# Attention reads the turned x back from DRAM, and the K projection is split around the second sums

## The chip, the cores and the metric

The kernel runs on one core of one Trainium2 chip. Its time is the device time of one execution in microseconds; lower is better. Three timed runs of the kernel before are shown, and one more execution was taken with the hardware profiler.

## What is computed

One decoder layer in float32 with 64 sequences of 128 tokens, width D = 256, 16 heads of 16. Three blocks, each with a residual and a layer norm behind it. Cut to what matters:

```python
# recurrence, per token t, with x [64, 128, 256]
q, k, v = x @ Wq, x @ Wk, x @ Wv;  g = sigmoid(x @ Wf + bf)
state = state * g + v outer k;      out = state @ q
out = layernorm(out) * gamma + beta
x1 = layernorm(x + (out * silu(x @ Wg)) @ Wout)
# cross attention with ctx [64, 128, 256]
Q, K, V = x1 @ Wxq.T + bq, ctx @ Wxk.T + bk, ctx @ Wxv.T + bv
x2 = layernorm(x1 + (softmax(Q K^T / 4) V) @ Wxo.T + bo)
# feed-forward with fake quantization: its outputs are scaled and rounded by the maximum over all tokens
x3 = layernorm(x2 + ffn(x2))
```

## The kernel before, in words

Three blocks of code follow one another, with all engines meeting between them: `recurrence_block`, `attention_block`, `feedforward_block`. In each block every engine has a program of its own, written out by hand, and the engines wait for one another on semaphores (counters). Within an engine the instructions run strictly in the written order, so a wait holds up everything behind it on that engine. There is no scheduler.

The first two blocks work on pairs of sequences, 32 pairs (`NP`). A matmul contracts over the partitions, so x has to be turned (features on the partitions, tokens along the row) before it is multiplied with a weight.

- The recurrence loads x of pair p into `rec_x`, turns it on TensorE (`turn`, four 128x128 transposes into a PSUM bank), and ScalarE copies the result to `rec_xT` (`turned`). The second sequence of a pair lies in `rec_x` and `rec_xT` with its four chunks of 32 tokens in reverse order (`place`). The result `rec_o` goes to the DRAM tensor `rec_scratch` (`store`), one DMA of 128 rows and four of 32.
- Attention loads three tiles of a pair in `load`: `att_x` from the input x, `att_ctx` from the context, `att_o` from `rec_scratch`. All three count up one semaphore of the slot, `a_loaded`, by 16 each. There are two slots. SyncE (SP) issues the load of a pair into a slot once `x1` of the pair that used the slot two pairs earlier is ready, that is, when VectorE has written both halves of `att_x1`.

In attention a step p handles the front half of pair p (gate, output of the recurrence, x1, K and V of the context) and the scores, softmax and output of pair p-1. TensorE's order in a steady step, by its helpers: turn x of pair p (`turn4(F[0], xs)`), turn the normalized recurrence output (`on`), the sums and values of the second sequence left from the step before (`values(n0-1)`: matmuls of the exponentials with ones and with V; "the second sums" are these), turn x1 of pair p-1, K projection of pair p (`across(F[1], wx[:, 1], cT)`), query projection, output projection (`att_out`), scores, gate projection (`across(F[2], w_g, xT)`), V projection, the second pass over the scores (`probs`, which needs the row maxima of VectorE through a transpose of `mparts`), the product with `w_out` (which needs `att_yT` of VectorE), scores, sums and values of the other sequence, the turn of the next context, `probs`, `att_out`.

VectorE's order in a step: `att` (the quotient of the sequence before), `stats_o` and `apply_o` of the pair p+1 (they read `att_o`, so they wait for `a_loaded`), `residual` and `stats2`, `maxima` of the first sequence, the gate's product `att_yT`, V, residual, `maxima` of the second sequence, `att`, statistics of x1, `residual`, and `apply`, which writes `att_x1` and so frees the slot for the next load.

Of the kernel before, what the change touches and what calls it, by code (L numbers as in the profile page):

```python
# [24 lines left out]
P = 128  # L25
# [47 lines left out]
def recurrence_block(nc, t, w, x_d, o_d):  # L73
# [25 lines left out]
    with ExitStack() as ctx:  # L99
# [60 lines left out]
        stored = [sem(f"rec_stored{i}") for i in range(2)]  # L160
        names = """marked consts consts_ready x_made xT_ready vf_made v_ready z_ready ez_ready lg_ready h_ready n_ready q_made q_ready
# [31 lines left out]
        with nc.Block() as block:  # L193

            @block.sync
            def _(sp):
# [12 lines left out]

                for s in range(2):  # L210
                    sp.sem_inc(stored[s], DMAS)
# [19 lines left out]
                sp.wait_ge(q["x_made"], 1)  # L231
                load(2, 0)
# [5 lines left out]
                sp.wait_ge(q["x_made"], NP - 2)  # L238
                load(NP - 1, 1)
                for p in range(NP - 4, NP):  # L240
                    store(p, p % 2)
                sp.wait_ge(qw["rest_loaded"], 16 * 12)
# [262 lines left out]
            def _(act):  # L505
# [245 lines left out]
def attention_block(nc, t, x_d, ctx_d, o_d):  # L751
# [3 lines left out]
    with ExitStack() as ctx:  # L755
# [12 lines left out]
        xT = sb("att_xT", [P, KC, 2 * P])  # L768
# [38 lines left out]
        names = """xT_made xT_ready cT_made cT_ready x1T_made x1T_ready q_made q_ready zg_made th_ready sg_ready  # L807
# [25 lines left out]
        with nc.Block() as block:  # L833

            @block.sync
            def _(sp):
                def load(pair, slot):
                    two = bass.ds(2 * pair, 2)
                    for dst, src in ((xs, x_d), (cs, ctx_d), (os_, o_d)):
                        sp.dma_start(dst[:, slot], src[two].rearrange("b t d -> t b d")).then_inc(a_loaded[slot], 16)  # L840

                load(0, 0)
                load(1, 1)
                with sp.Fori(0, (NP - 2) // 2) as j:
                    for u in range(2):
                        sp.wait_ge(q["x1_ready"], 2 * (2 * j + 1 + u))
                        load(2 * j + 2 + u, u)

            @block.tensor
            def _(pe):  # L850
# [12 lines left out]
                def across(bank_, wt, rhs, done):  # L863

                    for oc in range(KC):
# [3 lines left out]
                    m.then_inc(done, 1)  # L869
# [72 lines left out]
                def turn_context(p, s, before):  # L942
                    pe.wait_ge(a_loaded[s], 48 * (before + 1))
                    wait_if(pe, q["v_ready"], p)
                    turn4(F[1], cs[:, s], q["cT_made"])

                def step(p, s, before, front, attn, tail):
# [3 lines left out]
                    if front:  # L951
                        pe.wait_ge(a_loaded[s], 48 * (before + 1))
# [31 lines left out]
                    if front:  # L984
                        pe.wait_ge(q["ogb_ready"], 2 * p + 2)
                        pe.wait_ge(q["xT_ready"], p + 1)
                        across(F[2], t["w_g"], xT, q["zg_made"])
# [21 lines left out]
            def _(act):  # L1009
# [27 lines left out]
                def step(p, s, before, front, attn, tail):  # L1037
                    n0 = 2 * p - 2
                    if front:
                        act.wait_ge(q["xT_made"], p + 1)  # L1040
                        A.activation(flat(xT), F[0][:], ACT.Copy).then_inc(q["xT_ready"], 1)
# [42 lines left out]
            def _(dve):  # L1084
# [86 lines left out]
                def stats_o(p, s, before):  # L1171
                    dve.wait_ge(a_loaded[s], 48 * (before + 1))
# [743 lines left out]
def decoder_layer(nc, x_d, ctx_d, w, out_d):  # L1916

    with ExitStack() as ctx:
# [6 lines left out]
        r_d = nc.dram_tensor("raw_scratch", (NT, P, FC * 512), F32).ap()  # L1925
        g_d = nc.dram_tensor("gate_scratch", (NT, P, FC * 512), F32).ap()
# [9 lines left out]
        with ExitStack() as early:  # L1936
# [16 lines left out]
            recurrence_block(nc, t, w, x_d, o_d)  # L1953
            attention_block(nc, t, x_d, ctx_d, o_d)
# [28 lines left out]
```

## Time and profile before

| | us |
|---|---|
| median of 3 timed runs | 2223.21 (2216.39 to 2224.17) |
| profiled execution | 2219.33 |
| its span in the trace | 2217.6 |
| TensorE busy | 2007.4, 91% of the span |
| VectorE busy | 1582.9, 71% |
| ScalarE busy | 1268.4, 57% |
| mean granted TensorE clock | 0.962 of full speed |

The recurrence ends at about 772 us of the span, attention runs from about 773 to 1545 us, and the feed-forward block fills the rest. The profile names an engine's instruction by its line and by the tiles it writes and reads (out<-in). A number in square brackets behind a row is the time in which the engine stood idle before that row, with the instruction that ended the wait. PE is TensorE, PEld its weight loads, DVE VectorE, ACT ScalarE, POOL GpSimd, SPq the DMAs that SyncE issues. A float32 matmul shows as two records, a float32 transpose as one.

### The profile page before, as it was taken

The page shows a single profiled execution, that of the slowest core. Times are in us where ns is not written, and L with a number is a line of the kernel's source. Part 1 is how long each engine was busy: PE and PEld are TensorE (multiplying, and loading weights), DVE is VectorE, ACT ScalarE, POOL GpSimd, SP SyncE. Part 2 cuts the span into 40 slices and gives each one's busy share as a digit, 9 for nine tenths or more (in the row PEclk, how much of TensorE's full clock was granted, in tenths as well). Part 3 has the DMA queues.
Part 4 walks back from the last instruction along what each step waited for, and adds up shares of the span by engine and source line. Part 5 has one row for each costly group of instructions (what it writes and reads, how often), then busy time and mean ns, then how long its engine had stood idle before and what let it go on. Part 6 is the DMA issues. An engine that isn't in the chain of part 4 may idle for free. (4 is left out here: it accounts for less than half of the span.)

```text
span 2217.6 us, 72815 instructions
## 1 busy us (share of the span) xinstructions
PE 2007.4 (91%) x29431; PEld 1367.3 (62%) x29431; DVE 1582.9 (71%) x2810; ACT 1268.4 (57%) x2047; POOL 314.4 (14%) x313
## 2 busy tenths in 40 slices
PE   7999999999999789999999999997777877889798
PEld 4666666666666567777777777775333423334587
DVE  6787867777677757677677776775333379988897
ACT  4445444544445356766767667664544467678565
POOL 1231100101010111111111111110000022300021
PEclk9899999999999889999999999998888989999999
DMA  3001010100100010100101001000222368869574
GB/s 115 22 24 30 22 32 22 32 22 26 28 22 27 26 48 30 43 28 28 43 28 42 29 28 43 28 29 1 103 119 119 142 245 309 292 261 424 211 265 161
DMA packets 87527, 196.80 MB, mean 89 GB/s; under 512 B 11059, under 2 KB 64566, under 8 KB 87350
## 3 DMA queue, kind: packets, MB, share of 16 engines
q1 hardware_dynamic: 87350, 194.03, 24.7%
q8 instruction: 161, 2.64, 0.5%
q14 instruction: 16, 0.13, 0.0%
HBM read 108.01 MB, written 85.98 MB: 87 GB/s over the span
## 5 line engine op out<-in xcount | busy, mean ns | idle before, releaser
L1340 PE MATMUL ff_twin<-ff_xq,w_uh 128*128 (+1 forms) x1152 | 356.7, 392 | 42.7 <-DVE ff_top L1722 36.4
L1340 PEld LDWEIGHTS ff_twin<-ff_xq,w_uh 128*128 128x128 f16 x1152 | 113.5, 101 | 192.5 <-issue 55.4
L1340 PE MATMUL ff_twin<-ff_xq,w_ul 128*128 (+1 forms) x576 | 224.0, 389 | 0.0
L537 ACT ACTIVATE x<-rec_e,rec_hidden 128x512 f32<-128x512 f32 x256 | 156.0, 702 | 36.6 <-PE rec_e L372 36.6
L1119 DVE TENSOR_REDUCE mneg<-att_s 128x4 f32<-128x512 f32 x256 | 159.0, 684 | 17.8 <-PE att_s L894 17.1
L653 DVE TENSOR_TENSOR x<-rec_x,rec_until 128x512 f32<-128x512 f32 x256 | 158.8, 683 | 17.8 <-PE rec_x L356 17.8
L384 PE MATMUL rec_x<-x 32*32 32x64 f32 x8192 | 147.0, 219 | 18.1 <-DVE x L653 12.1
L384 PEld LDWEIGHTS rec_x<-x 32*32 32x32 f32 x8192 | 126.2, 107 | 54.6 <-issue 54.5
L1732 DVE TENSOR_REDUCE ff_top<-ff_out 128x1536 f32 (+1 forms) x32 | 56.1, 1754 | 137.0 <-ACT ff_out L1473 137.0
L1022 ACT ACTIVATE att_e<-att_s 128x512 f32<-128x512 f32 x256 | 132.2, 602 | 36.5 <-PE att_s L914 36.5
L333 PE MATMUL rec_f<-w_rec,rec_xT 128*128 128x512 f32 x256 | 134.9, 652 | 5.6 <-DVEq L586 4.5
L341 PE MATMUL rec_f<-rec_xT,w_rec 128*128 128x256 f32 x512 | 138.2, 404 | 0.9 <-ACT rec_v L519 0.9
L1782 DVE TENSOR_TENSOR ff_out<-ff_whole,s_other 128x1536 f32<-128x1536 int16 x64 | 115.0, 1802 | 27.3 <-ACT s_other L1527 14.0
L689 DVE TENSOR_TENSOR rec_tmp<-rec_x,x 32x256 f32<-32x256 f32 (+1 forms) x192 | 80.8, 421 | 75.2 <-PE rec_x L412 50.4
L289 POOL TENSOR_TENSOR rec_o<-rec_tmp 128x512 f32<-128x512 f32 x32 | 41.1, 1283 | 632.1 <-DVE rec_tmp L706 632.1
L1241 POOL TENSOR_TENSOR rs<-mv,half_pow 128x1 f32<-128x1 f32 (+1 forms) x96 | 57.8, 602 | 477.4 <-DVE mv L1163 379.1
L683 DVE TENSOR_TENSOR rec_tmp<-rec_x,x 128x512 f32<-128x512 f32 x128 | 83.8, 683 | 50.1 <-PE rec_x L384 49.9
L537 ACT ACTIVATE x<-rec_e 128x512 f32<-128x512 f32 x64 | 38.1, 597 | 131.6 <-PE rec_e L372 131.6
L341 PEld LDWEIGHTS rec_f<-rec_xT,w_rec 128*128 128x128 f32 x512 | 90.8, 192 | 33.3 <-issue 11.0
L1786 DVE TENSOR_REDUCE ff_topg<-ff_out 128x1536 f32 (+1 forms) x64 | 110.0, 1741 | 0.2 <-DVE ff_coef L1770 0.2
L1340 PEld LDWEIGHTS ff_twin<-ff_xq,w_ul 128*128 128x128 f16 x576 | 57.8, 100 | 72.1 <-issue 9.7
L676 DVE TENSOR_TENSOR x<-x,rec_v 128x2048 f32<-128x2048 f32 x32 | 73.3, 2291 | 37.4 <-ACT x L537 37.4
(250 smaller groups left out, 4481.7 us busy)
## 6 DMA issues: line engine op xcount, KB each, us to landing
raw_scratch<-ff_out SPq DMA_DIRECT2D x32, 768.0 KB, 3.2
ff_in<-raw_scratch SPq DMA_DIRECT2D x32, 768.0 KB, 6.0
gate_scratch<-ff_out SPq DMA_DIRECT2D x28, 768.0 KB, 3.6
ff_in<-gate_scratch SPq DMA_DIRECT2D x28, 768.0 KB, 9.1
product_scratch<-ff_out SPq DMA_DIRECT2D x28, 768.0 KB, 8.6
ff_out<-product_scratch SPq DMA_DIRECT2D x28, 768.0 KB, 6.2
att_x<-in_x SPq DMA_DIRECT2D x32, 256.0 KB, 2.7
att_ctx<-in_ctx SPq DMA_DIRECT2D x32, 256.0 KB, 2.9
```

What stands on the lines that cost most here:

```text
L333: T.matmul(bank_[:], xT[:, kc, b * P:(b + 1) * P], wr[:, kc, 2:4].rearrange("p a d -> p (a d)"), start=(kc == 0), stop=False)
L341: m = T.matmul(bank_[:, oc * 2 * P:(oc + 1) * 2 * P], wr[:, kc, i, oc * P:(oc + 1) * P], xT[:, kc], start=(kc == 0), stop=(kc == KC - 1))
L384: m = T.matmul(X[k][rows(c), h * NR * HD:(h + 1) * NR * HD].rearrange("p (r i) -> p r i", r=NR), mt[rows(c), b, hd, rows(c)], e[rows(c), s ...
L537: A.activation(out, E[(s + k) % 2][:], ACT.Exp, bias=hidden[:, asks, r:r + 1] if r < NR else 0.0, scale=-1.0 if asks else 1.0).then_inc(q[ ...
L653: V.tensor_tensor(mt[:, b].rearrange("p (a j m) n -> p j a m n", a=KC, m=2)[:, j], X[j].rearrange("p (a m n) -> p a m n", a=KC, m=2), unti ...
L683: V.tensor_tensor(tmp[:, k * HH:(k + 1) * HH, 0:NR], X[k].rearrange("p (h r i) -> p h r i", r=NR, i=HD), um[:, s, :, k * HH * HD:(k + 1) * ...
L689: V.tensor_tensor(tmp[lanes, b * H:(b + 1) * H, k], bank_[lanes, b * D:(b + 1) * D].rearrange("p (h i) -> p h i", i=HD), e[lanes, s, k, b ...
L1022: A.activation(e[:, b, j], X[j][:], ACT.Exp).then_inc(q["e_ready"], 1)
L1119: V.tensor_reduce(mneg[:, 4 * j:4 * j + 4], X[j].rearrange("p (h k) -> p h k", h=4), AX.X, ALU.max, negate=True).then_inc(q["s_taken"], 1)
L1340: m = T.matmul(bank_[:], weights(wp, kc, a, c), tile[:, xp, kc], start=(i == 0), stop=(i == len(terms) - 1))
L1782: V.tensor_tensor(ob[:, u, s], whole[:, u, s], other[:, s], ALU.mult).then_inc(q["prod"], 1)
L1786: V.tensor_reduce(topg[:, bass.ds(2 * k + s, 1)], ob[:, u, s], AX.X, ALU.max, apply_absolute_value=True).then_inc(q["maxed"], 1)
```

## The change

1. The recurrence writes each `rec_xT` to a new DRAM tensor `turned_scratch` (`keep`): one DMA for the first sequence (256 pieces of 512 bytes) and four for the chunks of the second, put back in order of time (256 pieces of 128 bytes each). ScalarE's copy of the next turned x waits until these have landed (`xT_out`). SyncE's order is now load, keep, store.
2. Attention no longer turns x nor copies it to `att_xT`. `load` gets a fourth DMA that reads the turned x, 128 rows of 2 KB, into a double-buffered place inside `raw_down`, a tile that is not in use then. It counts up the same semaphore, so all waits on `a_loaded` go from 48 to 64 a round.
3. Of the K projection of the next pair, the first of the two output chunks now stands ahead of `values(n0-1)`, the second stays behind the turn of x1.

```diff
+                def keep(pair):
+                    sp.wait_ge(q["xT_ready"], pair + 1)
+                    kept = xt_d[bass.ds(pair, 1)].rearrange("a p k n -> (a p) k n")
+                    sp.dma_start(kept[:, :, 0:P], xT[:, :, 0:P]).then_inc(xT_out, 16)
+                    for chunk in range(NC):
+                        at = place(1, chunk)
+                        sp.dma_start(kept[:, :, P + CH * chunk:P + CH * (chunk + 1)],
+                                     xT[:, :, P + CH * at:P + CH * (at + 1)]).then_inc(xT_out, 16)
...
                 with sp.Fori(0, NP // 2 - 2) as j:
                     for u in range(2):
-                        sp.wait_ge(q["x_made"], 2 * j + u + 2)
-                        load(2 * j + 3 + u, 1 - u)
+                        sp.wait_ge(q["x_made"], 2 * j + u + 3)
+                        load(2 * j + u + 4, u)
+                        keep(2 * j + u + 2)
                         store(2 * j + u, u)
...
                 def turned(p):
                     act.wait_ge(q["x_made"], p + 1)
+                    wait_if(act, xT_out, DMAS * p)
...
                     for dst, src in ((xs, x_d), (cs, ctx_d), (os_, o_d)):
                         sp.dma_start(dst[:, slot], src[two].rearrange("b t d -> t b d")).then_inc(a_loaded[slot], 16)
+                    sp.dma_start(xT[:, slot], xt_d[bass.ds(pair, 1)].rearrange("a p k n -> (a p) k n")).then_inc(a_loaded[slot], 16)
...
                     if front:
-                        pe.wait_ge(a_loaded[s], 48 * (before + 1))
-                        if attn and not tail:
-                            pe.wait_ge(q["xT_ready"], p)
-                        turn4(F[0], xs[:, s], q["xT_made"])
+                        pe.wait_ge(a_loaded[s], 64 * (before + 1))
...
                         turn4(F[2], on, q["onT_made"])
+                        pe.wait_ge(q["cT_ready"], p + 1)
+                        across(F[1], wx[:, 1], cT, q["k_made"], range(1))
                     if tail:
                         values(n0 - 1, s, 1)
                     if attn:
                         pe.wait_ge(q["x1_ready"], 2 * p)
-                        if front:
-                            pe.wait_ge(q["xT_ready"], p + 1)
                         turn4(F[0], x1, q["x1T_made"])
                     if front:
-                        pe.wait_ge(q["cT_ready"], p + 1)
-                        across(F[1], wx[:, 1], cT, q["k_made"])
+                        across(F[1], wx[:, 1], cT, q["k_made"], range(1, KC))
...
                 def stats_o(p, s, before):
-                    dve.wait_ge(a_loaded[s], 48 * (before + 1))
+                    dve.wait_ge(a_loaded[s], 64 * (before + 1))
```

How it moves instructions shows at three places. First TensorE at the start of a steady attention step, up to the query projection. Before (in the names, `att_x` stands for x and for x1):

```order
531 L859 MATMUL att_f<-ident,att_x 128x128 x4
532 L958 REGISTER_ALU
533 L859 MATMUL att_f<-ident,att_on 128x128 x4
534 L69 REGISTER_ALU
535 L921 ISA
536 L924 MATMUL att_a<-att_e,ones_half 32x256 x8
537 L930 MATMUL att_a<-att_e,v_half 32x128 x16
538 L966 REGISTER_ALU
539 L859 MATMUL att_f<-ident,att_x 128x128 x4
540 L867 MATMUL att_f<-att_cT,w_x 128x256 x4
541 L874 MATMUL att_f<-att_x1T,w_x 128x256 x4
```

The same place of the changed kernel:

```order
531 L876 MATMUL att_f<-ident,att_on 128x128 x4
532 L976 REGISTER_ALU
533 L884 MATMUL att_f<-att_cT,w_x 128x256 x2
534 L69 REGISTER_ALU
535 L939 ISA
536 L942 MATMUL att_a<-att_e,ones_half 32x256 x8
537 L948 MATMUL att_a<-att_e,v_half 32x128 x16
538 L876 MATMUL att_f<-ident,att_x 128x128 x4
539 L884 MATMUL att_f<-att_cT,w_x 128x256 x2
540 L892 MATMUL att_f<-att_x1T,w_x 128x256 x4
```

The first four transposes, those of x, are gone, and two of the four matmuls of the K projection have moved ahead of the sums.

Second SyncE in the attention loop, one pair's load. Before:

```order
92 L840 ISA
93 L840 DMA att_x<-in_x 128x2x256
94 L840 DMA att_ctx<-in_ctx 128x2x256
95 L840 DMA att_o<-rec_scratch 128x2x256
96 L840 ISA
```

And now (`raw_down` is where the turned x lies):

```order
122 L856 ISA
123 L856 DMA att_x<-in_x 128x2x256
124 L856 DMA att_ctx<-in_ctx 128x2x256
125 L856 DMA att_o<-rec_scratch 128x2x256
126 L857 ISA
127 L857 DMA raw_down<-turned_scratch 128x512
```

The fourth DMA stands last, behind that of `att_o`.

Third SyncE at the start of the recurrence, behind the weights. Before:

```order
25 L198 DMA rec_x<-in_x 128x256
26 L200 DMA rec_x<-in_x 32x256 x4
27 L233 UNCONDITIONAL_BRANCH
28 L233 ISA
29 L198 ISA
30 L198 DMA rec_x<-in_x 128x256
```

And now:

```order
26 L201 DMA rec_x<-in_x 32x256 x4
27 L214 DMA turned_scratch<-rec_xT 256x1x128
28 L217 DMA turned_scratch<-rec_xT 256x1x32 x4
29 L199 DMA rec_x<-in_x 128x256
30 L201 DMA rec_x<-in_x 32x256 x4
```

The five DMAs that write the turned x of pair 0 come behind the load of pair 2 and ahead of that of pair 3.

## Rows read from the trace of the kernel before

**Rows 1.** Windows: busy us of PE, PEld, DVE, ACT, POOL; granted clock; DMA.
```profile
20.00:740.00 720.00, 673.56 (x16410) 469.82 (x16410) 546.97 (x760) 345.82 (x602) 104.95 (x69) 0.98 0.10 26
800.00:1500.00 700.00, 688.59 (x8698) 519.23 (x8696) 497.33 (x1344) 478.97 (x870) 111.77 (x149) 1.00 0.11 33
```

**Rows 2.** Timeline of PE in attention: start, us, instruction, idle before it.
```profile
1101.79 1.89 PE L867 MATMUL att_f<-att_cT,w_x 128*128 128x256 f32 x8
...
1113.07 1.99 PE L882 MATMUL att_f<-w_out,att_yT 128*128 128x256 f32 x8
...
1120.38 1.13 PE L939 MATMUL att_a<-w_x,att_attT 128*128 128x256 f32 x4
1121.35 0.60 PE L859 MATMUL att_f<-ident,att_x 128*128 128x128 f32 x4
1121.79 0.60 PE L859 MATMUL att_f<-ident,att_on 128*128 128x128 f32 x4
1122.59 1.07 PE L924 MATMUL att_a<-att_e,ones_half 128*32 128x256 f32 x16 [0.20 <-ACT att_e L1022]
```

**Rows 3.** Timeline of DVE in the same step.
```profile
1104.31 0.75 DVE L1158 BATCH_NORM_STATS2 st_o<-att_o 128x6 f32<-128x256 f32 x2 [0.95 <-DMA att_o<-rec_scratch]
...
1111.31 0.23 DVE L1125 TENSOR_TENSOR mparts<-mneg,mparts 128x64 bf16<-128x64 f32 x1
...
1112.32 0.69 DVE L1202 TENSOR_TENSOR att_yT<-att_silu,att_ogb 128x512 f32<-128x512 f32 x1 [0.19 <-DVE att_silu L1198]
...
1121.89 0.73 DVE L1168 TENSOR_SCALAR att_x<-att_res,mv,rs 128x256 f32<-128x256 f32 x2
```

**Rows 4.** Timeline of SP, loads of two pairs in attention.
```profile
1100.09 0.42 SPq L840 DMA_DIRECT2D att_ctx<-in_ctx  x1
1100.61 0.42 SPq L840 DMA_DIRECT2D att_o<-rec_scratch  x1
...
1123.80 0.42 SPq L840 DMA_DIRECT2D att_o<-rec_scratch  x1
```

**Rows 5.** DMA issues of the page: count, KB each, median us from issue to landing.
```profile
att_ctx<-in_ctx SPq DMA_DIRECT2D x32, 256.0 KB, 2.9
att_o<-rec_scratch SPq DMA_DIRECT2D x32, 256.0 KB, 3.6
...
rec_scratch<-rec_o SPq DMA_DIRECT2D x128, 32.0 KB, 1.6
```

**Rows 6.** A window of 0.4 us while three tiles arrive; last columns DMA share, GB/s.
```profile
1124.60:1125.00 0.40, 0.40 (x5) 0.40 (x5) 0.35 (x1) 0.40 (x1) 0.00 (x0) 1.00 1.09 364
```

**Rows 7.** Timeline of DVE and PE in a step whose `att_o` landed early.
```profile
1126.99 0.75 DVE L1158 BATCH_NORM_STATS2 st_o<-att_o 128x6 f32<-128x256 f32 x2 [0.46 <-DMA att_o<-rec_scratch]
...
1136.13 1.99 PE L882 MATMUL att_f<-w_out,att_yT 128*128 128x256 f32 x8
```

**Rows 8.** The tile `att_o`: what its readers waited for (us, times), and landing.
```profile
  DMA att_o<-rec_scratch: 35.8, 31
...
DMA to landing us min/median/max: 3.0/3.6/4.8
```

**Rows 9.** Timelines of SP and ACT in a steady step of the recurrence.
```profile
418.32 3.34 SPq L200 DMA_DIRECT2D rec_x<-in_x  x4
...
440.68 0.63 ACT L511 ACTIVATE rec_xT<-rec_f 128x512 f32<-128x512 f32 x1
```

**Rows 10.** Timelines at the start of the recurrence: SP, ACT, PE.
```profile
21.77 1.35 SPq L200 DMA_DIRECT2D rec_x<-in_x  x3
...
26.15 0.63 ACT L511 ACTIVATE rec_xT<-rec_f 128x512 f32<-128x512 f32 x1
...
26.92 1.96 PE L333 MATMUL rec_f<-w_rec,rec_xT 128*128 128x512 f32 x4 [1.12 <-ACT rec_xT L511]
```

**Rows 11.** Windows at the end of attention, columns as in rows 1.
```profile
1520.00:1530.00 10.00, 8.15 (x90) 5.50 (x83) 6.02 (x15) 3.50 (x8) 0.77 (x2) 1.00 0.00 0
1530.00:1540.00 10.00, 9.33 (x136) 7.06 (x125) 3.33 (x7) 4.92 (x10) 0.00 (x0) 0.66 0.01 2
```

More of the change, by code:

```diff
@@ L69, in wait_if, with recurrence_block @@
         eng.wait_ge(sem, value)
-def recurrence_block(nc, t, w, x_d, o_d):
+def recurrence_block(nc, t, w, x_d, o_d, xt_d):
     NP = B // 2
@@ L160, in recurrence_block @@
         stored = [sem(f"rec_stored{i}") for i in range(2)]
+        xT_out = sem("rec_xT_out")
         names = """marked consts consts_ready x_made xT_ready vf_made v_ready z_ready ez_ready lg_ready h_ready n_ready q_made q_ready
@@ L230, in _ @@
                     sp.dma_start(t[dst][:], w[dst].partition_broadcast(P)).then_inc(qw["rest_loaded"], 16)
-                sp.wait_ge(q["x_made"], 1)
-                load(2, 0)
+                for p in range(2):
+                    sp.wait_ge(q["x_made"], p + 1)
+                    load(p + 2, p)
+                    keep(p)
                 with sp.Fori(0, NP // 2 - 2) as j:
                     for u in range(2):
-                        sp.wait_ge(q["x_made"], 2 * j + u + 2)
-                        load(2 * j + 3 + u, 1 - u)
+                        sp.wait_ge(q["x_made"], 2 * j + u + 3)
+                        load(2 * j + u + 4, u)
+                        keep(2 * j + u + 2)
                         store(2 * j + u, u)
-                sp.wait_ge(q["x_made"], NP - 2)
-                load(NP - 1, 1)
-                for p in range(NP - 4, NP):
+                for p in range(NP - 2, NP):
+                    keep(p)
+                    store(p - 2, p % 2)
+                for p in range(NP - 2, NP):
                     store(p, p % 2)
+                sp.wait_ge(xT_out, DMAS * NP)
                 sp.wait_ge(qw["rest_loaded"], 16 * 12)
@@ L746, in _, with attention_block @@
                 weights()
-def attention_block(nc, t, x_d, ctx_d, o_d):
+def attention_block(nc, t, x_d, ctx_d, o_d, xt_d):
     NP = B // 2
@@ L767, in attention_block @@
         os_ = sb("att_o", [P, 2, 2, D])
-        xT = sb("att_xT", [P, KC, 2 * P])
+        xT = t["raw_down"].rearrange("p c d -> p (c d)")[:, 0:4 * KC * P].rearrange("p (s k n) -> p s k n", s=2, k=KC)
         cT = sb("att_cT", [P, KC, 2 * P])
@@ L861, in turn4, with across @@
                     m.then_inc(done, 1)
-                def across(bank_, wt, rhs, done):
-                    for oc in range(KC):
+                def across(bank_, wt, rhs, done, chunks=range(KC)):
+                    for oc in chunks:
                         for kc in range(KC):
@@ L868, in across @@
                                          rhs[:, kc], start=(kc == 0), stop=(kc == KC - 1))
-                    m.then_inc(done, 1)
+                    if chunks[-1] == KC - 1:
+                        m.then_inc(done, 1)
                 def query(p, oc):
@@ L951, in step @@
                     if front:
[L952 to L955 removed]
+                        pe.wait_ge(a_loaded[s], 64 * (before + 1))
                         if isinstance(p, int) and p == 0:
@@ L985, in step @@
                         pe.wait_ge(q["ogb_ready"], 2 * p + 2)
-                        pe.wait_ge(q["xT_ready"], p + 1)
-                        across(F[2], t["w_g"], xT, q["zg_made"])
+                        across(F[2], t["w_g"], xT[:, s], q["zg_made"])
                         pe.wait_ge(q["k_ready"], 2 * p + 2)
@@ L1925, in decoder_layer @@
         r_d = nc.dram_tensor("raw_scratch", (NT, P, FC * 512), F32).ap()
+        xt_d = nc.dram_tensor("turned_scratch", (B // 2, P, KC, 2 * P), F32).ap()
         g_d = nc.dram_tensor("gate_scratch", (NT, P, FC * 512), F32).ap()
@@ L1952, in decoder_layer @@
             })
-            recurrence_block(nc, t, w, x_d, o_d)
-            attention_block(nc, t, x_d, ctx_d, o_d)
+            recurrence_block(nc, t, w, x_d, o_d, xt_d)
+            attention_block(nc, t, x_d, ctx_d, o_d, xt_d)
         feedforward_block(nc, t, r_d, g_d, u_d, out_d)
```

4 lines of the change are left out of this document (1 added, 3 removed).

## The prediction

> **What bounds the kernel now.** I read the windows by stage first. From 800 to 1500 us, attention, TensorE is busy 688.6 of 700 us at a granted clock of 1.00; the recurrence has it busy 673.6 of 720 us [rows 1]. So attention looks bound by TensorE alone, and every matmul taken out of it looks like time won. The timelines of a step then tell more. A steady step takes about 23.3 us. On TensorE I follow it from the end of `att_out`, 1120.38 + 1.13 = 1121.51 [rows 2]. There VectorE adds the residual and writes x1, done at 1121.89 + 0.73 = 1122.62 [rows 3]; this frees the slot, and SP issues the three loads, the one of `att_o` at 1123.80 [rows 4]. VectorE's next large piece starts with the statistics of that same `att_o`, and it stood idle for the DMA: 0.95 us in the step shown [rows 3], 35.8 us in 31 of 32 steps [rows 8]. So the load comes too late for VectorE in every step. VectorE works in order, and behind this wait stand the maxima (`mparts`, done at 1111.54) and the gate's product `att_yT` (1112.32 + 0.69 = 1113.01) [rows 3]. TensorE starts the product with `w_out` at 1113.07, 0.06 us after `att_yT` [rows 2, 3]. There is a second loop beside TensorE's own: x1, load, statistics, maxima, `att_yT`, `w_out`, the rest of the step, x1.
>
> Which of the two sets the pace shows in steps whose load landed at different times. In the usual step VectorE starts on `att_o` 3.70 us after its issue (1100.61 to 1104.31) and `w_out` follows 8.76 us later, 12.46 after the issue [rows 2 to 4]. In a step with an early landing it starts 3.19 us after the issue (1123.80 to 1126.99), but `w_out` comes 9.14 us after that, 12.33 after the issue [rows 4, 7]. So 12.33 is TensorE's own path and 12.46 that of the load. Of the 30 steps whose load is issued inside the loop, 25 keep a distance of at most 8.88 us from the start of `st_o` to `w_out` (like the first pair of rows) and five have 0.1 to 0.4 us more (like the second): the load's loop binds in 25, TensorE in five, and the two lie 0.13 us apart. That is the whole argument: TensorE is full, but not alone in setting the end.
>
> **The change part by part.** All sums are against the profiled execution, 2219.3 us (span 2217.6), which lies 3.9 us under the median of the runs, 2223.2.
>
> Turn of x removed: the four transposes hold TensorE for 1121.79 - 1121.35 = 0.44 us a step [rows 2]. ScalarE's copy to `att_xT` (0.6 us) goes too; ScalarE isn't late there. Half K projection ahead of the sums: two of four matmuls, half of 1.89 us [rows 2], moved and not saved. It covers the 0.20 us that TensorE waits for the exponentials today [rows 2], since it lasts longer than the turn that it replaces. TensorE's own path thus shrinks by 0.64 us, from 12.33 to 11.69. What is late next is the load's loop at 12.46, so of the 0.64 us nothing arrives, save in the five steps in which TensorE was last: about 0.3 us each, 1.5 us in all.
>
> The fourth load: it is issued last, about 0.5 us behind that of `att_o` (the pitch of 1100.09 to 1100.61 [rows 4]), and VectorE's statistics now wait for it as well, though they don't read it. While the three tiles arrive the DMA moves 364 GB/s, its share 1.09 [rows 6]. 256 KB more take 262 / 364 = 0.72 us at that rate. If the queue were not full, the fourth would land by its issue pitch later, 0.5 us. If it came as `att_o` comes behind `att_ctx`, it would be 0.52 + 3.6 - 2.9 = 1.2 us [rows 4, 5]. I take 0.7: the windows show a full stream, and the rate is what a further tile meets. Nothing hides it, because VectorE already idles at this wait, and everything from there to `w_out` is the fixed 8.76 us. 30 steps by 0.7 are 21.0 us; less the 1.5 us above, 19.5.
>
> (The Trainium skill, DMA: Bandwidth & Descriptors, section Anatomy of one DMA, fits a DMA as a fixed part plus its bytes at 436 GB/s. By that 256 KB add 0.60 us, and the term would be 18.0 instead of 21.0. The rate in rows 6 is lower, and the estimate above goes by it.)
>
> The first pairs of attention wait for their first load in the open; the fourth DMA adds 0.7 us once. The last step with a front half has no load behind it, and there the 0.64 us are won once.
>
> Writing the turned x, steady part: SP has issued its load by 418.32 + 3.34 = 421.66; five more DMAs at the same 0.84 us take it to 425.9, and with the 1.6 us that a 32 KB store needs to land they are there by about 427.5 [rows 5, 9]. ScalarE's next copy, which now waits for them, starts at 440.68 [rows 9]: 13 us to spare. The store of `rec_o` behind them in SP's queue waits for GpSimd's result until near the end of the step anyway, and its slot is needed two steps later. Cost 0. Without that cover each us of lateness would cost ScalarE's copy, and TensorE behind it, one.
>
> Writing it, start: SP ends the load of pair 2 at 21.77 + 1.35 = 23.12 [rows 10]. Five DMAs at about 0.5 us bring the last issue to 25.2, and landing 1.6 us or more later gives 27 [rows 5]. The copy of pair 1 starts at 26.15 today, and TensorE already waits for it [rows 10], so this delay is open. I take 1.0 us, between 0 and 2.5.
>
> Sum: 19.5 + 0.7 - 0.6 + 1.0 = **20.6 us slower**: 2239.9 for an execution like the profiled one, 2243.8 from the median. I say 2243.
>
> **The rivals.**
> (a) TensorE's path decides, as the share of 98% says. Place: the start of each step; price: 0.64 us by 31 steps, 20 us, so 2203, faster. It decides alone only if the load's loop gets 0.77 us shorter than today, since only then is 11.69 the longer path. For it speaks nothing but the busy share; against it the 0.06 us between `att_yT` and `w_out`, and that the change adds to the load rather than taking from it.
> (b) The fourth tile costs nothing: it lands together with `att_o` because that one is slow for a reason of its own (its landing varies from 3.0 to 4.8 us [rows 8]), and the DMA has room. Then the loop stays at 12.46, 1.5 + 0.6 us are won and 1.0 lost: 2222, no change. Against it the full rate [rows 6].
> (c) The clock. TensorE will idle some 1.2 us more a step, most of it ahead of the second pass over the scores. After 10 us with TensorE 8.15 us busy the clock granted in the next 10 was 0.66, which is a drop to the lower of the two levels for part of them [rows 11]. A drop costs 0.34 by 10 = 3.4 us of matmul time. If it came in half of the steps it would add 15 by 3.4 = 51 us: 2294. Against it: the steps would still be about 94% busy, and the recurrence runs at 673.6 / 720 = 94% with 0.98 granted [rows 1].
> (d) The small pieces written in the recurrence are slow and hold up ScalarE's copy in every step. 1280 pieces a pair are 80 for each of 16 DMA engines; to use up 13 us each would need over 0.16 us. A piece of 1 KB takes 16 KB / 364 GB/s = 0.05 us [rows 6]. At twice the limit, each step would lose 13 us and the kernel would be at 2600. (The Trainium skill, same page, section Specifications, says that pieces under 512 bytes are read, changed and written back, and gives no price. At double the 0.05 us the sum stays as it is.)
>
> **How the numbers follow.** Forecast 0.70, (b) or a tile that costs less than 0.35 us 0.15, (a) 0.06, (c) 0.06, (d) 0.03. The forecast's own range by the bounds of the fourth tile: 30 by 0.5 less 1.5 with a start of 0 gives 13.6 us, 2237; 30 by 1.2 less 1.5 with a start of 2.5 gives 37 us, 2261. To hold 8 in 10, the range has to take in most of (b): 2224 to 2262. About 0.5%, 11 us, is what a measurement of this kernel can tell from no change. Slower by more than that (over 2234): the forecast with (c) and (d), 0.77. Within it: (b) and a small part of the forecast, 0.17. Faster: 0.06.
>
> **What would show it.** Right: VectorE's idle time ahead of `st_o` grows from 0.95 to about 2.0 us a step (0.7 of the tile, 0.3 because ScalarE, rid of a copy, lets VectorE come to it sooner) and is put down to the new DMA; the distance from `att_o`'s issue to `w_out` goes from 12.46 to about 13.2, that from the start of `st_o` to `w_out` stays 8.76; attention's TensorE share falls from 98% to about 94%, with idle time ahead of the second pass over the scores (`mneg`, `mparts`) and ahead of `w_out`; its clock stays 1.00; the recurrence, from 60 to 740 us, keeps its length. Wrong: a period of attention below 23.3 us, or a tile landing under 0.35 us after `att_o`, or a clock under 0.98 in attention, or ScalarE waiting for `turned_scratch` beyond the first steps.

## The result, and the profile after

The changed kernel takes 2267.5 us (median of 4 runs, 2254.6 to 2271.8), against 2219.8 for the kernel before (4 runs, 2211.5 to 2224.2). The ratio is 1.021, with a 95% interval of 1.0153 to 1.0266. It is slower, as forecast, but by about 47 us where 20.6 were forecast, and the time lies outside the range, whose upper end was 2262. A second measurement of the same kernel (the first experiment below) confirms the size.

First the windows by stage, with the columns of rows 1.

```profile
60.00:740.00 680.00, 641.39 (x15702) 447.74 (x15700) 512.99 (x707) 322.58 (x560) 104.47 (x68) 0.97 0.15 36
800.00:1500.00 700.00, 689.22 (x8048) 500.86 (x8046) 464.15 (x1259) 434.29 (x791) 104.41 (x139) 0.98 0.14 44
```

TensorE's busy share in attention is 689.2 of 700, as high as the 688.6 of rows 1. By this number alone nothing has happened. But it did fewer matmuls in that time (8048 against 8698, 7.5% less, while the removed transposes are only 4 of some 290 in a step), and the clock is 0.98 instead of 1.00. Short waits inside a group of matmuls are counted as busy, as shown below, so this share can't show the longer loop. The counts and the timelines can.

The loads of one pair, from SP's timeline, then VectorE's timeline of the same step:

```profile
1123.10 0.37 SPq L856 DMA_DIRECT2D att_x<-in_x  x1
1123.57 0.42 SPq L856 DMA_DIRECT2D att_ctx<-in_ctx  x1
1124.09 0.42 SPq L856 DMA_DIRECT2D att_o<-rec_scratch  x1
1124.69 0.34 SPq L857 DMA_DIRECT2D raw_down<-turned_scratch  x1
```

```profile
1129.08 0.75 DVE L1169 BATCH_NORM_STATS2 st_o<-att_o 128x6 f32<-128x256 f32 x2 [2.66 <-DMA raw_down<-turned_scratch]
...
1136.07 0.23 DVE L1136 TENSOR_TENSOR mparts<-mneg,mparts 128x64 bf16<-128x64 f32 x1
1137.09 0.69 DVE L1213 TENSOR_TENSOR att_yT<-att_silu,att_ogb 128x512 f32<-128x512 f32 x1 [0.19 <-DVE att_silu L1209]
```

These answer to rows 3 and 4. VectorE comes to the statistics and idles 2.66 us for the new DMA. What the readers of `att_o` wait for, and when that tile itself has landed:

```profile
  DMA raw_down<-turned_scratch: 81.9, 31
...
DMA to landing us min/median/max: 3.4/3.7/4.7
```

VectorE waited 35.8 us in 31 steps [rows 8]; now it is 81.9 us, all of it put down to the fourth tile. The 3.7 us for `att_o` are no proof that this tile lands as before: all four DMAs count on one semaphore, and landings are read from its counts.

TensorE's timeline over two steps:

```profile
1107.96 2.49 PE L926 MATMUL att_s<-att_qm,att_kT 32*128 32x256 f32 x8
...
1111.73 3.55 PE L900 MATMUL att_f<-w_out,att_yT 128*128 128x256 f32 x8 [0.25 <-DVE att_yT L1213]
...
1134.07 2.49 PE L926 MATMUL att_s<-att_qm,att_kT 32*128 32x256 f32 x8
...
1137.83 1.99 PE L900 MATMUL att_f<-w_out,att_yT 128*128 128x256 f32 x8 [0.25 <-DVE att_yT L1213]
```

In the second step `w_out` starts at 1137.83, 8.75 us after `st_o` at 1129.08: the fixed distance of the prediction. The group of L926 is the first half of the second pass over the scores, eight matmuls that wait for VectorE's maxima (`mneg`). They take 2.49 us; in the kernel before they take 0.71, because `mneg` is there already:

```profile
1111.29 0.71 PE L908 MATMUL att_s<-att_qm,att_kT 32*128 32x256 f32 x8
```

The 1.8 us between the two lengths are idle time, but not one idle stretch. TensorE gets two matmuls at a time, one pair for each `mneg`, 0.6 us apart. Its weight loads show the waits, and a window over the same time counts PE as fully busy, because each matmul's record lasts 0.37 to 0.48 us and reaches over the wait behind it:

```profile
1108.56 0.29 PEld L926 LDWEIGHTS att_s<-att_qm,att_kT 32*128 32x128 f32 x2 [0.30 <-DVE mneg L1130]
1109.16 0.29 PEld L926 LDWEIGHTS att_s<-att_qm,att_kT 32*128 32x128 f32 x2 [0.31 <-DVE mneg L1130]
...
1108.00:1110.50 2.50, 2.50 (x9) 1.23 (x9) 2.43 (x6) 0.00 (x0) 0.00 (x0) 1.00 0.00 0
```

I call this the thin stretch. In the first step the product with `w_out` (L900) takes 3.55 us instead of 1.99, and two windows of 4 us show why:

```profile
1108.00:1112.00 4.00, 3.75 (x34) 2.14 (x35) 3.74 (x9) 0.78 (x3) 0.00 (x0) 1.00 0.00 0
1112.00:1116.00 4.00, 4.00 (x32) 2.84 (x35) 1.76 (x5) 2.84 (x5) 0.00 (x0) 0.57 0.00 0
```

From 1112 to 1116 us, shortly behind the thin stretch, the granted clock is 0.57, so for most of them it was at the lower of the two levels (1.2 of 2.4 GHz). The trace has nine such drops in the attention loop, and each comes 3.4 to 4.2 us after the start of this group, about when `w_out` begins.

I measured both distances of the prediction over all 30 loads issued inside the loop. From the issue of `att_o` to the start of `st_o` it is 3.71 us on average before and 4.82 after. From `st_o` to `w_out` it is 8.76 or 8.88 in 23 of 30 steps before and in 27 after. From `st_o` to the issue of the next `att_o` it is between 19.4 and 19.7 in most steps of both; after the change it is about 21.2 in 8 of 29, and in the first step, which has the ninth drop, 19.65, where the first and the fifth experiment below, without a drop there, have 17.96. So the 52.2 us by which the profiled executions differ (span 2269.8 against 2217.6) are made up as follows. The loop, from the first to the last of these issues, holds 29 steps and is 44.1 us longer. Its third line is what the first two leave; the filled kernel below, without a drop, has 2.6 there.

| place | us |
|---|---|
| recurrence, with its start | +1.8 |
| attention loop, `st_o` starts later behind the issue: 29 × 1.10 | +31.9 |
| attention loop, nine clock drops: 9 × 1.65 | +14.9 |
| attention loop, the rest: steps that TensorE had bound, and a shorter first step | −2.7 |
| first pair of attention | +1.1 |
| behind the last load, 3.8 of it in feed-forward | +5.3 |

The first line of the table can't be told from nothing: the six traces here whose recurrence is the unchanged one reach attention between 767 and 773 us.

### The profile page after: what moved, and what is told of

It is laid out like the page before. It is cut to its first block and busy times, and to the rows that moved or that the text cites. A ratio compares the mean times of both kernels' runs of the same rounds, so it can differ in the third digit from the quotient of the medians.

```text
span 2269.8 us, 73055 instructions
## 1 busy us (share of the span) xinstructions
PE 2057.5 (91%) x29303; PEld 1378.4 (61%) x29303; DVE 1581.0 (70%) x2810; ACT 1250.1 (55%) x2015; POOL 314.7 (14%) x313
## 5 line engine op out<-in xcount | busy, mean ns | idle before, releaser
L1351 PE MATMUL ff_twin<-ff_xq,w_uh 128*128 (+1 forms) x1152 | 361.3, 397 | 43.6 <-DVE ff_top L1733 35.2
L926 PE MATMUL att_s<-att_qm,att_kT 32*128 32x256 f32 x1024 | 148.1, 430 | 3.2 <-DVE mneg L1130 2.9
```

The source lines that it names most:

```text
L926: T.matmul(X[j][:, oc * 2 * P:(oc + 1) * 2 * P].rearrange("p (m q) -> p m q", m=2), kT[rows(j), s, oc, toks], qm[rows(j), oc, :, toks], st ...
L1351: m = T.matmul(bank_[:], weights(wp, kc, a, c), tile[:, xp, kc], start=(i == 0), stop=(i == len(terms) - 1))
```

## The experiments

Ratios are against the kernel before, run beside each experiment on the same chip. "Lag" is the mean from the issue of `att_o` to the start of `st_o`; "loop" is from the first to the last of these loads' issues, 676.5 us before and 720.6 after.

**The changed kernel once more.** No edit.

> The changed kernel itself, once more, beside the others of this chip: 44 to 52 us slower than the kernel before. The clock theory expects again some 6 to 12 of the 30 loop steps to be 1.6 us longer than the rest, and mean granted clock in attention 0.97 to 0.99.

2261.7 us, ratio 1.0207 (1.0172 to 1.0242). Lag 4.74, loop 715.4, seven clock drops in it, each in a step of 21.2 to 21.4 us, and the clock of attention again below 1:

```profile
800.00:1500.00 700.00, 690.28 (x8062) 503.05 (x8060) 468.05 (x1269) 433.52 (x789) 105.51 (x141) 0.98 0.14 43
```

Both parts of the loss in the loop are there again, so neither is an accident of one execution.

**The turned x on a semaphore of its own.** The load is the same, but only TensorE waits for it, right ahead of the gate projection.

```diff
-sp.dma_start(xT[:, slot], ...).then_inc(a_loaded[slot], 16)
+sp.dma_start(xT[:, slot], ...).then_inc(t_loaded[slot], 16)
-dve.wait_ge(a_loaded[s], 64 * (before + 1))    # statistics; the same for TensorE's turns
+dve.wait_ge(a_loaded[s], 48 * (before + 1))
+pe.wait_ge(t_loaded[s], 16 * (before + 1))
 across(F[2], t["w_g"], xT[:, s], q["zg_made"])
```

> The changed kernel, with one thing altered: the load of the turned x counts up a semaphore of its own, on which TensorE waits ahead of the gate projection; VectorE's statistics wait for three tiles as before the change. All the traffic and TensorE's new order stay. Theory (the fourth tile at VectorE's wait costs about 1.1 us a step, and the clock drops that follow from TensorE idling cost the rest): from the issue of att_o to the start of its statistics 3.7 us again instead of 4.8, steps of about 23.2 us, granted clock in attention 0.99 to 1.00, in all within 5 us of the kernel before. Rival (the writes to DRAM in the recurrence, the missing turn or the split K projection cost by themselves): it stays 20 to 50 us slower than the kernel before.

2228.3 us, ratio 1.0093 (1.0057 to 1.0128). More than half of the loss goes once VectorE's statistics no longer wait for a tile that they don't read. It doesn't go altogether: 17 us are left by the medians and 21 by the ratio, so the expectation, within 5 us, was missed. The loop is 8.3 us longer than before (684.8) and the lag is 4.00; the rest lies outside the loop and is not broken down. One step of the loop is long, though the clock of attention rounds to 1.00. The page's DMA issues, with size and median time to landing, say what is left:

```profile
att_o<-rec_scratch SPq DMA_DIRECT2D x32, 256.0 KB, 4.0
raw_down<-turned_scratch SPq DMA_DIRECT2D x32, 256.0 KB, 4.0
```

Here the three tiles that VectorE waits for are alone on their semaphore, so the landing can be trusted: `att_o` lands at 4.0 instead of 3.6 [rows 5]. The only thing new near it is the fourth tile issued behind it. 29 × 0.29 = 8.4 us is the loop's 8.3; the long step and the steps that TensorE had bound cancel. The group of the second pass lasts 1.7 us in the median step here. In the long step it is 1.81, and `w_out` behind it runs as slowly as in the changed kernel:

```profile
1223.43 1.81 PE L927 MATMUL att_s<-att_qm,att_kT 32*128 32x256 f32 x8
...
1226.52 3.60 PE L901 MATMUL att_f<-w_out,att_yT 128*128 128x256 f32 x8 [0.25 <-DVE att_yT L1215]
```

**The fourth load alone.** The kernel before, with its own turn of x and its own K projection, loads 256 KB more from an input.

```diff
+sp.dma_start(fourth[:, slot], x_d[two].rearrange("b (u r) d -> (b u) (r d)", r=2)).then_inc(a_loaded[slot], 16)
-dve.wait_ge(a_loaded[s], 48 * (before + 1))    # the same for TensorE
+dve.wait_ge(a_loaded[s], 64 * (before + 1))
```

> The kernel before, with a fourth DMA of 256 KB in rows of 2 KB behind that of att_o (it reads x again, into raw_down, and nothing uses it), counted by the same semaphore, so that all waits are for 64. TensorE's work is that of before. Theory: att_o's statistics start about 4.8 us after its issue instead of 3.7, which gives 30 x 1.1 less 1.5 = 31 us more, and if the clock drops come with it up to 15 us besides. If a tile from an input lands sooner than one from a scratch tensor, the lag is 4.4 (by the DMA's rate) and the cost 20 us. Rival (the tile's landing isn't what costs): within 5 us of the kernel before.

2243.5 us, ratio 1.0153 (1.0125 to 1.0182), 32 us slower. The lag is 4.78 and the loop 703.8, which is 27.3 more. So this wait is bought by the load alone, whatever else the change does, and a tile from an input costs what one from scratch costs. What this run does not show are long steps: there are none, and the clock is 1.00.

```profile
800.00:1500.00 700.00, 686.38 (x8366) 511.87 (x8366) 476.91 (x1291) 460.26 (x837) 107.53 (x143) 1.00 0.14 44
```

Its TensorE timeline has the turn of x back, and with it a shorter thin stretch in the second pass over the scores (here L910), 1.69 us where it was 2.49:

```profile
1116.52 1.69 PE L910 MATMUL att_s<-att_qm,att_kT 32*128 32x256 f32 x8
...
1119.48 1.99 PE L884 MATMUL att_f<-w_out,att_yT 128*128 128x256 f32 x8 [0.24 <-DVE att_yT L1204]
```

**The fourth load, made small.** As above, with 8 KB instead of 256, in pieces of 64 bytes.

```diff
-sp.dma_start(fourth[:, slot], x_d[two].rearrange(...)).then_inc(a_loaded[slot], 16)
+sp.dma_start(fourth[:, slot, 0:16], x_d[two].rearrange(...)[:, 0:16]).then_inc(a_loaded[slot], 16)
```

> As the kernel before with a fourth DMA, but that DMA carries 8 KB (64 bytes a row) instead of 256 KB. It tells what of the 1.1 us is the issue and completion of one more DMA and what its bytes. If the fourth DMA costs by its bytes alone, as the prediction's 0.7 us assumed: the lag from att_o's issue to its statistics is 3.7 to 3.8 us, total within 3 us of the kernel before. If half a microsecond is the issue behind att_o's: lag 4.1 to 4.3, total 12 to 17 us more, and the 256 KB of the full tile account for the other 0.6 us.

2221.0 us, ratio 1.0046 (1.002 to 1.0071), 7 to 10 us slower. The lag is 4.00 and the loop 681.5. This lies between the two expectations, so neither is right by itself: of the 1.07 us that the fourth load costs, 0.29 come with one more DMA even if it carries next to nothing (the run doesn't tell which of the four then lands last, nor what pieces of 64 bytes do to it), and 0.78 with its bytes (4.78 less 4.00). The prediction's 0.7 was the price of the bytes.

**Filling TensorE's thin stretch.** The changed kernel, with twelve more transposes of the identity in each step between the V projection and the second pass over the scores, into a bank that isn't read.

```diff
 along(F[1], cT, wx[:, 2], q["v_made"])
+if attn:
+    for _ in range(12):
+        T.transpose(F[0][:, 2 * P:3 * P], ident[:], ident[:])
```

> The changed kernel with 12 transposes of the identity more in each step, 1.3 us of TensorE work that nothing uses, between the V projection and the second pass over the scores, where TensorE now stands idle for VectorE's maxima. Clock theory: the idle stretch gets too short for a drop, the long steps vanish, granted clock 1.00 in attention, and the kernel is 10 to 18 us faster than the changed kernel although it does more. Rival (the long steps have another cause than TensorE's idling, for example the larger load): the same time as the changed kernel or up to 5 us more, and the long steps stay.

2249.4 us, ratio 1.0153 (1.0122 to 1.0185). It does more work than the changed kernel and is 12 us faster than it was on the same chip (2261.7). The two intervals touch at their ends (1.0122 to 1.0185, 1.0172 to 1.0242); what settles it are the steps. The lag is the same (4.82), but no step is long: no distance from `st_o` to the next issue is above 19.83, and the trace has no clock drop in the loop. The loop is 705.6 us, 9.8 less than in the changed kernel's second trace and 15 less than in its first.

```profile
1120.51 1.47 PE L1005 MATMUL att_f<-ident 128*128 128x128 f32 x12
1121.91 1.17 PE L926 MATMUL att_s<-att_qm,att_kT 32*128 32x256 f32 x8
```

```profile
800.00:1500.00 700.00, 691.72 (x8548) 526.39 (x8550) 478.10 (x1295) 438.90 (x801) 106.69 (x143) 1.00 0.13 42
```

The transposes hold TensorE for 1.47 us, so that it comes to the second pass later and finds most of `mneg` there; the pass shrinks from 2.49 to 1.17, and the clock is back at 1.00. The clock loss is thus real and comes from that stretch.

**Only the writing.** The recurrence of the changed kernel, which writes the turned x, with the attention of the kernel before.

```diff
-attention_block(nc, t, x_d, ctx_d, o_d, xt_d)
+attention_block(nc, t, x_d, ctx_d, o_d)      # as before the change
```

> The recurrence of the changed kernel, which writes the turned x to DRAM, with attention as before the change, which doesn't read it. Theory: one delay of 1 to 2 us at the start, nothing in the steady part: 1 to 3 us slower than the kernel before. Rival (the small pieces cost in every step): 10 us or more.

2217.8 us, ratio 1.0027 (1.0006 to 1.0049), 4 to 6 us more. The attention loop is 676.35 us, as before. The trace shows one wait for these DMAs, at the start, on ScalarE:

```profile
28.52 0.60 ACT L527 ACTIVATE rec_xT<-rec_f 128x512 f32<-128x512 f32 x1 [1.48 <-DMA turned_scratch<-rec_xT]
```

It starts at 28.52 instead of 26.15 [rows 10], and in the changed kernel at 27.19. In steady steps the 1024 pieces of 128 bytes that each pair writes cost nothing that shows: from the fourth of these copies to the last it is 638 to 649 us in the seven traces that write them and 640 to 647 in the six that don't. The expected 1 to 3 us lie inside the interval, and so does the rival's 10 us, near its upper end (1.3 to 10.8 us); it is the loop and these copies that speak against the rival.

**Only the split of the K projection.** The kernel before, with half of the K projection ahead of the sums.

```diff
+pe.wait_ge(q["cT_ready"], p + 1)
+across(F[1], wx[:, 1], cT, q["k_made"], range(1))       # ahead of the sums
...
-across(F[1], wx[:, 1], cT, q["k_made"])
+across(F[1], wx[:, 1], cT, q["k_made"], range(1, KC))   # behind the turn of x1
```

> The kernel before with only the first half of the K projection moved ahead of the second sums. Theory: TensorE's wait for the exponentials ahead of the sums (0.2 us a step) is covered, its own path falls to 12.1 us, and since the load's loop binds at 12.46 in most steps the gain is what the five early landings leave: 0 to 2 us less. Rival (it starves ScalarE of the turned x1 and costs a wait for it): 5 us more or worse.

2216.3 us, ratio 1.0002 (0.9979 to 1.0026). The loop is 673.7 us, 2.8 less, and the time is the same. TensorE's own path got shorter where the load's loop decides, and that is worth nothing measurable.

**`att_o` first, in the kernel before.** `att_o` is issued ahead of the other tiles and has its own semaphore, for which alone the statistics wait.

```diff
-for dst, src in ((xs, x_d), (cs, ctx_d), (os_, o_d)):
+for dst, src, done in ((os_, o_d, o_loaded), (xs, x_d, a_loaded), (cs, ctx_d, a_loaded)):
...
-dve.wait_ge(a_loaded[s], 48 * (before + 1))
+dve.wait_ge(o_loaded[s], 16 * (before + 1))
```

> The kernel before with only the order and the semaphore of the loads altered: att_o first, awaited alone by VectorE's statistics. x is turned on TensorE as before. Theory: the load's loop leaves the bound, TensorE's own 12.33 us take its place of 12.46: 25 x 0.13 = 3 us less, with no idle time of VectorE ahead of st_o. Rival (the load's loop had more in it than TensorE's path): 10 us less or more.

2206.5 us, ratio 0.9981 (0.996 to 1.0002), 4 us less. The loop is 671.7 us, 4.8 less or 0.17 us a step (the median period goes from 23.25 to 23.17). This is the other half of the test of the two loops: with the load out of the way TensorE's own path sets the pace. The prediction had the two paths 12.46 and 12.33 us long, 0.13 apart. From the last of the three issues, where `att_o`'s used to be, to `w_out` it is now 12.33 on average.

**`att_o` first, in the changed kernel.** The same edit on top of the own semaphore for the turned x.

> As the run with the semaphore of its own, and att_o is now loaded first, with a third semaphore, on which alone VectorE's statistics wait. Theory: the load's loop gets at least 0.95 us shorter than in the kernel before (VectorE's idle time there), about 11.5 us against 11.7 of TensorE's own path, so that TensorE binds and the removed turn pays at last: 25 x 0.77 + 5 x 0.64 = 22 us less, 2 us of it given back at the start of the recurrence, so about 20 us under the kernel before; idle time of VectorE ahead of st_o goes to zero. Rival (another wait of the step is just as long, for example between w_out and the end of att_out): within 5 us of the kernel before.

2191.3 us, ratio 0.9911 (0.9884 to 0.9938), 20 us faster than before and, by the ratios (1.021 and 0.9911), some 66 us less than the change as it was made. The tile's waits and landing, VectorE's statistics, and the window:

```profile
  DMA att_o<-rec_scratch: 4.3, 3
...
DMA to landing us min/median/max: 2.5/2.7/4.9
```

```profile
1152.58 0.74 DVE L1172 BATCH_NORM_STATS2 st_o<-att_o 128x6 f32<-128x256 f32 x2
```

```profile
800.00:1440.00 640.00, 638.29 (x8176) 478.36 (x8175) 474.73 (x1280) 436.62 (x796) 105.31 (x141) 1.00 0.14 46
1160.28 0.71 PE L928 MATMUL att_s<-att_qm,att_kT 32*128 32x256 f32 x8
```

VectorE waits for this tile in 3 steps instead of 31. The eight matmuls of the second pass take 0.71 us: this is what they need when nothing is missing, so the 2.49 of the changed kernel held 1.8 us of waiting. The median period is 22.46, 0.79 less than before; the prediction's two paths are 12.46 − 11.69 = 0.77 apart. Now the saved TensorE time arrives, as in rival (a), whose condition this edit brings about.

**The same, with the K projection whole.**

```diff
-across(F[1], wx[:, 1], cT, q["k_made"], range(1))       # ahead of the sums
...
+pe.wait_ge(q["cT_ready"], p + 1)
+across(F[1], wx[:, 1], cT, q["k_made"])                 # behind them, as before
```

> The kernel with att_o first and semaphores of its own, and the turned x from DRAM, but with the K projection whole again behind the turn of x1. With the turn of x gone and nothing in its place TensorE reaches the second sums 0.44 us sooner and waits 0.64 us for ScalarE's exponentials instead of 0.2. Theory: each step loses what the half projection covered, 0.6 us, less what VectorE's loop leaves: 15 to 20 us slower than the version with the split, so close to the kernel before (within 8 us). Rival (the split does nothing): the same as with the split, 20 us under the kernel before.

2214.5 us, ratio 0.9998 (0.9977 to 1.002); by the ratios this is 19 us slower than with the split. The median period is 23.16, that of the kernel before with `att_o` first. The turn of x is gone and nothing is gained, since TensorE comes to the sums before the exponentials are there:

```profile
1157.68 1.07 PE L944 MATMUL att_a<-att_e,ones_half 128*32 128x256 f32 x16 [0.64 <-ACT att_e L1037]
```

It was 0.20 with the turn ahead of it [rows 2] and is 0.64 without. The half K projection is not an addition to the removed turn but what makes it count.

**`att_o` first and the K projection split, without the turned x.** The kernel before with both edits; x is turned on TensorE as it was.

> The kernel before, with att_o loaded first and awaited alone, and the K projection split, but without the turned x from DRAM. TensorE binds, and the split covers the wait for the exponentials: 0.2 us a step or 6 us less than with the order of loads alone, so 8 to 12 us under the kernel before. The turned x from DRAM would then be worth the remaining 0.44 to 0.5 us a step, 13 to 15 us, less 4 to 8 us that it costs at the start of the recurrence, in the first step and in the feed-forward block. Rival (the turned x is worth nothing): the same time as the version with all three, 20 us under the kernel before.

2194.3 us, ratio 0.9906 (0.9875 to 0.9937), not to be told from the 0.9911 above. So the total is the rival's: some 21 us under the kernel before, where 8 to 12 were expected. The median period is 22.90, 0.27 less than with `att_o` first alone, and the loop is 661.6 us against 649.4 with the turned x: in the loop the turned x does win, 0.44 us a step and 12 us in all. The timed runs don't show these 12 us. The two intervals are 12 and 14 us wide; 2.0 us go the other way in the feed-forward block (669.2 us there, 667.2 here), and the traces reach attention at 772.4 and 768.1, which is within the spread of one and the same recurrence (the result section). The row of the sums has no wait left:

```profile
1153.11 1.07 PE L926 MATMUL att_a<-att_e,ones_half 128*32 128x256 f32 x16
```

This is the simplest kernel that beats both: no DMA added, no scratch, two small edits. Whether the turned x is worth anything on top stays open.

## Why the prediction was right on the load's loop and wrong on the time

The forecast was 20.6 us; some 47 were measured. Two steps of it failed: the fourth tile was taken at 0.7 us a load and cost 1.1, and the sum had no term for the clock, which cost some 15 us.

**The load's loop decides: right.** `st_o` to `w_out` stayed 8.76 or 8.88 us in nearly every step, while the start of `st_o` moved. The 0.64 us taken from TensorE's path did not arrive in the changed kernel. With `att_o` first it does: the median period is 23.17 without and 22.46 with the other two edits, 0.71 less. The split alone, `att_o` first alone, and both together (0, 4 and some 20 us) show the two loops as they were put: 0.13 us apart, so that shortening either one alone gives little.

**The fourth tile: the term of the sum that was mis-sized.** The prediction had 30 × 0.7 = 21.0 us; measured were 30 × 1.11 = 33. The value lay inside the stated bounds of 0.5 to 1.2, so the choice between them failed, in two ways. It counted bytes only, and one more DMA costs 0.29 us even with 8 KB. And it took the rate of a window in which three tiles were under way as the rate that the last tile meets. In the changed kernel that rate holds for about 1 us:

```profile
1125.00:1125.50 0.50, 0.50 (x5) 0.50 (x6) 0.37 (x2) 0.41 (x2) 0.00 (x0) 1.00 1.04 365
...
1126.00:1126.50 0.50, 0.44 (x3) 0.03 (x2) 0.42 (x1) 0.47 (x2) 0.00 (x0) 1.00 0.62 207
1126.50:1127.00 0.50, 0.50 (x2) 0.47 (x3) 0.00 (x0) 0.50 (x2) 0.00 (x0) 1.00 0.83 262
1127.00:1127.50 0.50, 0.50 (x4) 0.34 (x4) 0.00 (x0) 0.31 (x1) 0.00 (x0) 1.00 0.82 285
```

The tail of the stream moves at 207 to 285 GB/s in this step. The kernel before had such a tail too, in the step of rows 2 to 4, and the prediction didn't read it:

```profile
1103.00:1103.50 0.50, 0.50 (x4) 0.31 (x3) 0.36 (x1) 0.39 (x1) 0.00 (x0) 1.00 0.63 213
```

Written with 1.1 the sum would have been 33 instead of 21 and the forecast 2255, inside the range; the upper estimate in the prediction, 1.2 from the landing times of `att_o` and `att_ctx`, was the nearer row. (The Trainium skill, DMA: Bandwidth & Descriptors, section Anatomy of one DMA, fits a DMA that GpSimd issues as 2.0 us and its bytes at 436 GB/s. By its rate 256 KB behind others would add 0.60 us, an estimate; the two runs with a fourth load give 0.78 for the bytes and 0.29 beside them. The measurement decides.)

**The clock: a step that failed outright.** Rival (c) had it right in kind, and the prediction gave it 0.06. Two errors. It was set up as a case instead of the forecast, while in fact it came on top of it: 9 steps of 29 at 1.65 us each, some 15 us, where (c) had supposed half the steps at 3.4. And the evidence against it was a mean. "About 94% busy, like the recurrence" says nothing of where the idle time lies; here it is packed into one stretch of 2.5 us that holds 0.7 us of work. Where that group lasts 2.5 us at most and 2.4 to 2.5 in the median, the two traces have nine and seven drops. Where it lasts 1.7 in the median, one trace (the turned x on its own semaphore) has two, one of them in the loop's first step behind a group of 2.49 us, and the other (the fourth load alone) none. The filled kernel, with the group at 1.2, has none and confirms the cause. Why only some of the thin stretches are followed by a drop, the runs don't tell.

The prediction named "a clock under 0.98 in attention" as a sign of being wrong. It was 0.98, just at the edge: 9 short drops hardly move a mean over 700 us. Distances within the step show them far better.

**TensorE's busy share: wrong.** It was forecast at 94% and stayed at 98%. The idle time lies inside the groups that wait for parts of their input, and the window above counts it as busy. **VectorE's idle time** was forecast at 2.0 us and is 2.66 in the step shown, and the distance from `att_o`'s issue to `w_out`, forecast at 13.2, is 13.6 on average: the mis-sized tile again.

**The recurrence: right, with luck in the number.** The steady part cost nothing, and rival (d) is out. The copy of pair 1 came at 27.19 instead of 26.15, 1.04 us later, against the 1.0 taken. But this trace shows no wait for the DMAs in front of it, and the same copy starts between 25.97 and 27.20 in the six traces that write nothing (26.6 on average) and between 26.34 and 28.52 in the seven that write (27.3):

```profile
22.82 2.62 SPq L217 DMA_DIRECT2D turned_scratch<-rec_xT  x4
...
27.19 0.60 ACT L527 ACTIVATE rec_xT<-rec_f 128x512 f32<-128x512 f32 x1
```

**Rivals (a) and (b)** are excluded by the lag. It grew by 1.11 us and `w_out` moved with it, so the tile isn't free and the load's loop still decides.

**What stays open: the feed-forward block.** It runs the same code in all kernels, yet by the timelines it takes 670.6 us after the change and 666.4 to 669.9 in the five other kernels that read a turned x from DRAM. It takes 666.8 before, 663.1 in the kernel with the fourth load alone, and 663.5 to 663.7 in four others without a turned x; the last experiment, also without one, has 667.2. The granted clock in its first 100 us is 0.84 to 0.85 in five of the six that read the turned x and in the last experiment, and 0.88 in all the others. The length goes with this clock and not with the turned x: 667.2 to 670.6 us at the lower value, 663.1 to 666.8 at 0.88. No experiment tells what sets it. The block's part in the loss is 3.8 of the 5.3 us of the table.

## What to carry to other kernels

An engine that the profile shows at 98% need not set the pace: look for the loop that closes through a load, and measure both loops in steps that differ. Before work is taken from TensorE, look where its waits will gather, since a mean busy share doesn't show it. Order the loads of a burst by who waits first, and give a tile with another reader its own semaphore; a tile added to a shared one is paid for by all its waiters. Then take work from the engine: here the edits gave 4 and 0 us apart and some 20 together.

## What the runs showed of the hardware

- One more DMA behind three of 256 KB, on the same semaphore, put off its completion by 0.29 us with 8 KB and by 1.07 us with 256 KB. With 256 KB on a semaphore of its own it still made the reader of the tile issued ahead of it start 0.29 us later.
- A stretch of 2.5 us in which TensorE had 0.7 us of matmuls, in pairs with waits of 0.3 us between their weight loads, was followed in 9 of 29 steps of a loop by a granted clock at the lower level, 0.57 over the next 4 us, and a step 1.65 us longer. In a second trace it was 7 of 29. With the same work in 1.7 us in the median step it was two drops in one kernel, one of them behind a stretch of 2.5 us, and none in another. Filling the time ahead of it with useless transposes removed the drops and made the kernel 12 us faster.
- 1024 pieces of 128 bytes a pair, written in the background of the recurrence, had no steady cost that shows: the whole kernel was 0.27% (0.06 to 0.49) slower, and the one wait for them in the trace is 1.48 us, at the start.
